# Node tables of 128 partitions, split first loads, and head sums one group later in a graph network kernel

## The reference

```python
h = relu(layernorm(x))
# first network: heads=8, head size 16
hn = layernorm(h) * g + b
fh, ft, fe = hn @ W_head.T, hn @ W_tail.T, hn @ W_ent.T
e = leaky_relu(fh[src] * ft[dst], 0.2)            # per edge
e = sum over a head's 16 of (e * attn) * log(deg[dst]) / 16
a = softmax of e over the edges of each dst
f = fe
for _ in range(5):                                 # hops
    agg = segment_sum(f[src] * a, dst)
    f = 0.85 * agg + 0.15 * fe
rst = f + h;  x = x + ff(layernorm(rst)) + rst     # ff: 128 -> 512 -> 128
# second network: three graph convolutions over the same edges with edge_weight
x = x + gcn3(relu(layernorm(x)))
```

## Time and profile before

| | |
|---|---|
| median of 3 runs | 6570.55 us |
| profiled execution | 6571.94 us |
| its span | 6570.2 us |
| granted TensorE clock, mean | 0.611 |
| PE busy | 4080.4 us, 62% |
| DVE busy | 3665.7 us, 56% |
| POOL busy | 3938.5 us, 60% |
| ACT busy | 423.4 us, 6% |
| DMA moved | 671.66 MB, 102 GB/s on average |

### The profile page before, as it was taken

One profiled execution on the slowest core, in us unless ns is written; L12 is line 12 of the kernel. 1 busy time (PEld: TensorE's weight loads), 2 busy tenths in 40 slices (PEclk: granted clock), 3 DMA queues, 4 the chain that ended last, 5 costly groups with the idle time before them and its releaser, 6 DMA issues.

```text
span 6570.2 us, 90031 instructions
## 1 busy us (share of the span) xinstructions
PE 4080.4 (62%) x19868; PEld 3634.8 (55%) x19869; DVE 3665.7 (56%) x7015; ACT 423.4 (6%) x1409; POOL 3938.5 (60%) x4073
## 2 busy tenths in 40 slices
PE   2755655625778998865555545555544555555899
PEld 1444544514668888854444534445544454544899
DVE  6765656787865555535555535555544555544211
ACT  0111111110000000000000000000000000001000
POOL 0577767711047777767777767777776777773000
PEclk9655555557965555555555555555555555566999
DMA  2345566514633323223233322332322333332576
GB/s 56 108 140 146 145 155 144 150 34 122 179 103 79 78 78 79 75 59 79 78 80 78 78 59 77 79 78 78 80 63 71 79 78 80 78 72 75 217 273 230
DMA packets 538440, 671.66 MB, mean 102 GB/s; under 512 B 102388, under 2 KB 423419, under 8 KB 528412
## 3 DMA queue, kind: packets, MB, share of 16 engines
q0 software_dynamic: 143008, 320.73, 18.8%
q1 hardware_dynamic: 391970, 345.94, 17.6%
q10 hardware_dynamic: 3418, 4.48, 0.2%
HBM read 511.17 MB, written 160.80 MB: 102 GB/s over the span
## 4 chain that ended last, share of the span: by engine, by line
POOL 30%; issue 22%; PE 21%; DMA 13%; DVE 9%; SPq 1%; DVEq 1%; ACT 1%; POOLq 0%; ACTq 0%; PEldq 0%; PEld 0%
POOL U L683 30%; DMA U<-tab_f,stage 9%; PE ps L888 7%; PE ps L1101 6%; PE ps L877 5%; DMA U<-edge_fe 2%; DVE gap L1168 2%; DVE U L1194 1%; DMA U<-tab_he,stage 1%; DVE U L1522 1%; DVE U L1494 1%; ACT stage L746 1%; DVEq L1168 1%; DVE U L1121 1%; PE ps L964 1%
## 5 line engine op out<-in xcount | busy, mean ns | idle before, releaser
L683 POOL DMA_INDIRECT U<-tab_f,stage x3224 | 3054.7, 947 | 1354.8 <-issue 865.6
L888 PE MATMUL ps<-U 128*125 128x128 f32 x8160 | 2012.3, 401 | 1075.7 <-DVE U L1194 1075.1
L888 PEld LDWEIGHTS ps<-U 128*125 128x125 f32 x8160 | 1672.7, 290 | 1209.4 <-issue 1209.1
L1194 DVE TENSOR_TENSOR U<-U,ex_it 128x512 f32<-128x512 f32 x1020 | 711.9, 698 | 1064.5 <-DMA U<-tab_f,stage 1062.9
L1145 DVE TENSOR_TENSOR U<-dloc,iota_p 128x500 f32<-128x500 f32 x1225 | 839.9, 686 | 535.0 <-DMA U<-tab_f,stage 478.0
L683 POOL DMA_INDIRECT U<-tab_he,stage x806 | 841.7, 1044 | 427.4 <-issue 244.8
L877 PE MATMUL ps<-gap 128*128 128x125 f32 x2816 | 723.9, 436 | 453.1 <-DVE gap L1168 452.5
L877 PEld LDWEIGHTS ps<-gap 128*128 128x128 f32 x2816 | 627.1, 328 | 539.7 <-DVE gap L1168 537.8
L1179 DVE SCALAR_TENSOR_TENSOR gap<-gap,U,ps 128x125 f32<-128x125 f32 x1408 | 485.6, 345 | 154.3 <-DVE gap L1179 42.6
L989 PE MATMUL ps<-U 125*128 x1632 | 422.3, 440 | 183.1 <-ACT U L783 181.3
L885 PEld LDWEIGHTS ps<-w_it,U 128*125 128x125 f32 x1632 | 439.1, 329 | 162.6 <-issue 162.5
(11 more groups left out here) (237 smaller groups left out, 2093.1 us busy)
## 6 DMA issues: line engine op xcount, KB each, us to landing
adj<-gap SPq DMA_DIRECT2D x1408, 64.0 KB
edge_fe<-U SPq DMA_DIRECT2D x204, 256.0 KB, 2.8
U<-edge_fe SPq DMA_DIRECT2D x204, 256.0 KB, 3.0
U<-tab_f,stage POOLq DMA_INDIRECT x3224, 2.5
ex_it<-adj SPq DMA_DIRECT2D x30, 1600.0 KB, 6.2
U<-adj SPq DMA_DIRECT2D x30, 1600.0 KB, 6.2
fe_a<-adj SPq DMA_DIRECT2D x15, 1600.0 KB, 6.2
U<-tab_he,stage POOLq DMA_INDIRECT x806, 3.1
```

The costliest lines, as they stand in the source:

```text
L683: pool.indirect_dma_start(to[:, k, j, :], None, table, bass.IndirectOffsetOnAxis(ap=stage[:, k, j:j + 1], axis=0)).then_inc(landed[k], 16)
L888: mm = nc.tensor.matmul(ps[0:BN, bass.ds(b * F, F)], hot[:, k, j, :], ga[:, k, j, :], start=False, stop=False, skip_group_check=True)
L1194: v.tensor_tensor(rows_, rows_, by, ALU.mult).then_inc(msgs_ready, 1)
```

## The change

Tables tab_he and tab_f get 128 x 25 rows. Row 25 p + b is now partition p of bucket b, so each partition's buckets lie together, and all 128 partitions are stored. The three that hold no node, with 29 others, are zeroed once by POOL. The source index of an edge is turned into the new row number by five more DVE operations. tab_f is stored in two parts, by SP after four banks' sums and by ACT after all seven. The copies to the sorted table and the loads of x are cut at a multiple of 16 rows; x, the constants and later the keys are loaded from ACT's queue. In the score stage a group's sum of heads is issued behind the next group's product.

```diff
-        tab_he = dram("tab_he", (N_NODES, 2 * F))
+        tab_he = dram("tab_he", (P * NB, 2 * F))
-        tab_f = dram("tab_f", (N_NODES, F))
+        tab_f = dram("tab_f", (P * NB, F))
+EVEN = BN // 16 * 16                 # 112
+EVEN_TILES = TILES // 16 * 16        # 768 of 782
+        def rows_of(table):
+            return table.rearrange("(p b) f -> p b f", p=P)
@@ sync, start
-                sp.dma_start(srt[:, k, :], of[0:TILES * P].rearrange("(t e) -> t e", e=P)).then_inc(edges_copied, 16)
-            sp.dma_start(h0[0:BN], nodes_of(a["x"])).then_inc(x_in, 16)
-            loads = [...]
-            for to, of in loads:
-                sp.dma_start(to, of, allow_slow_non_contiguous=True).then_inc(consts_in, 16)
+                for t0, t1 in ((0, EVEN_TILES), (EVEN_TILES, TILES)):
+                    sp.dma_start(srt[t0:t1, k, :], of[t0 * P:t1 * P].rearrange("(t e) -> t e", e=P)
+                                 ).then_inc(edges_copied, 16)
@@ scalar, start
+            for p0, p1 in ((0, EVEN), (EVEN, BN)):
+                act.dma_start(h0[p0:p1], nodes_of(a["x"])[p0:p1]).then_inc(x_in, 16)
+            loads = [...]
+            for to, of in loads:
+                act.dma_start(to, of, allow_slow_non_contiguous=True).then_inc(consts_in, 16)
@@ sync, keys
-            sp.wait_ge(rows_ready, 3)
+            sp.wait_ge(rows_ready, 2)
@@ sync, table
-            sp.dma_start(nodes_of(tab_he[:, 0:F]), na[0:BN]).then_inc(table_out, 16)
-            sp.dma_start(nodes_of(tab_he[:, F:2 * F]), x_sb[0:BN]).then_inc(table_out, 16)
+            sp.dma_start(rows_of(tab_he[:, 0:F]), na).then_inc(table_out, 16)
+            sp.dma_start(rows_of(tab_he[:, F:2 * F]), x_sb).then_inc(table_out, 16)
@@ key loads: the same 32 loads move from sync to scalar, before the same turns
-                        sp.dma_start(key[c * HEADS:(c + 1) * HEADS, :],
+                        act.dma_start(key[c * HEADS:(c + 1) * HEADS, :],
...
@@ sync, hop border
-                    for k in range(BANKS):
-                        b0, b1 = bank_buckets(k)
-                        sp.wait_ge(sums_out, n * BANKS + k + 1)
-                        sp.dma_start(nodes_of(tab_f)[:, b0:b1], na[0:BN, b0:b1]).then_inc(table_out, 16)
+                    b0, b1 = part_buckets(PARTS[0])
+                    sp.wait_ge(sums_out, n * BANKS + PARTS[0][1])
+                    sp.dma_start(rows_of(tab_f)[:, b0:b1], na[:, b0:b1]).then_inc(table_out, 16)
@@ scalar, hop border
             for s in range(1, HOPS):
+                b0, b1 = part_buckets(PARTS[1])
+                act.wait_ge(sums_out, s * BANKS)
+                act.dma_start(rows_of(tab_f)[:, b0:b1], na[:, b0:b1]).then_inc(table_out, 16)
                 stage_pass(s)
@@ scalar, before hop 0
-            act.dma_start(x_sb[0:BN], nodes_of(a["x"])).then_inc(x_again, 16)
+            for p0, p1 in ((0, EVEN), (EVEN, BN)):
+                act.dma_start(x_sb[p0:p1], nodes_of(a["x"])[p0:p1]).then_inc(x_again, 16)
@@ gpsimd
+            pool.wait_ge(slide_set, 1)
+            pool.memset(U[P - 32:P, 0:2 * NB * F], 0.0).then_inc(rest_set, 1)
+            pool.wait_ge(rest_set, 1)
@@ vector, row numbers
-                    v.tensor_copy(row_f[0], row_i[0]).then_inc(rows_ready, 1)
+                    link(v.tensor_copy(row_f[0], row_i[0]))
+                    link(v.tensor_scalar(row_b, row_f[0], -(BN - 1) / 2, 1.0 / BN, ALU.add, ALU.mult))
+                    link(v.tensor_scalar(row_b, row_b, ROUND, None, ALU.add))
+                    link(v.tensor_scalar(row_b, row_b, -ROUND, None, ALU.add))
+                    link(v.scalar_tensor_tensor(out=row_f[0], in0=row_b, scalar=-float(BN), in1=row_f[0], op0=ALU.mult,
+                                                op1=ALU.add))
+                    v.scalar_tensor_tensor(out=row_f[0], in0=row_f[0], scalar=float(NB), in1=row_b, op0=ALU.mult,
+                                           op1=ALU.add).then_inc(rows_ready, 1)
@@ vector, score stage
+            def reduce_scores(r, k):
+
+                dve.wait_ge(step_link, r * (3 * SLOTS) + (3 * k + 3))
+                v.tensor_reduce(ex_it[:, bass.ds(item_of(r, k), G), :],
+                                ga_wide[:, k % SLOTS, :, 0:F].rearrange("p g (h d) -> p g h d", h=HEADS),
+                                AX.X, ALU.add).then_inc(scores_done, 1)
+
                         v.tensor_tensor(heads, heads, bank(2 + k % 2).rearrange("p (g f) -> p g f", g=G),
                                         ALU.mult).then_inc(step_link, 1)
+                        if k or r0:
+                            reduce_scores(r, k - 1)
...
-                        dve.wait_ge(step_link, r * (3 * SLOTS) + (3 * k + 3))
-                        v.tensor_reduce(ex_it[:, bass.ds(item_of(r, k), G), :],
-                                        heads.rearrange("p g (h d) -> p g h d", h=HEADS),
-                                        AX.X, ALU.add).then_inc(scores_done, 1)
-
-            score_groups(0, WIN_COUNT_AT)
+
+            score_groups(0, 1)
+            score_groups(1, WIN_COUNT_AT)
...
             score_groups(FULL_ITERS, ITERS)
+            reduce_scores(ITERS - 1, SLOTS - 1)
```

66 lines of the change are left out of this document (36 added, 30 removed).

## The result

| | before | after |
|---|---|---|
| median | 6571.41 us (4 runs, 6566.51 to 6574.25) | 6490.49 us (4 runs, 6488.59 to 6491.5) |
| profiled span | 6570.2 us | 6489.3 us |
| POOL busy | 3938.5 us, 60% | 3899.4 us, 60% |
| granted TensorE clock, mean | 0.611 | 0.612 |

The ratio is 0.9876, with a 95% interval of 0.9864 to 0.9887: 81 us less (the 6570.55 us ahead of the prediction is the median of three of the four runs). I had forecast 6469 us, 102 less, with a range of 6438 to 6512.

The account below looks back on a forecast made before the run. POOL's gathers were taken as the clock of 5 of the 6.57 ms. Start -11, score stage -55, borders -33 and hop 0 -3 sum to -102 us: median 6469 us, range 6438 to 6512 (forecast alone 6440 to 6492).

Parts of the forecast that it names:

- Rival 1: Score stage: the long gather stays, by another cause or on another start; 60 us lost, 6529 us, chance 0.13.
- long compares: Score stage: three gathers slowed beside long DVE compares, said to stay long; 6 of the 70 us of slow gathering.
- Slow gathers: Score stage: reordered sums keep two-SBUF-input DVE operations off gather starts, group 5.04 instead of 5.42 us; 60 us gained.
- Look-ahead: Score stage: late sums shrink it by 3.4 of about 10 us; costs +3 at window count, +2 at first group.
- rival 2: Score stage, congested stretch: missed look-ahead lengthens each of five waits by 5.04 us; 6494 us, chance 0.12.
- Key loads on ACT: Score stage: eight issues hold ACT 2.6 us in four iterations, covered by look-ahead; taken as 0, range -12 to +12.
- The chain through ACT and PE: Score stage: product, reduction, ACT's stage and copy, PE's tails, next product; 4.53 us, under the group's 5.04.
- rival 3: Score stage: the new chain through ACT and PE becomes the clock; at 5.9 us a group 6621 us, chance 0.03.
- Borders: Four hop borders: stores from 128 partitions at 300 GB/s, 10.7 instead of 18.7 us each; -33 us (-22 to -39).
- Rival 4: Stores don't spread over more engines; borders and start give 5 instead of 44 us: 6508 us, chance 0.04.
- Start: Kernel start: DVE copies weights at 46.2 instead of 62.43 us, less added operations and later dst loads; -11 us (-13 to -5).
- Hop 0: First hop: x reloaded during its first loads, spread over all engines, delays them less; -3 us (0 to -6).

Follow-up runs that it names:

- e1: Changed kernel with each group's sum of heads back behind its own product instead of a group late: 6529.25 us, ratio 0.9930.
- e6: e1 with the next group's one-hots moved behind the product: 6605.53 us, ratio 1.0039.
- e4: Changed kernel with head sums in their own group and the leaky relu split into two operations through PSUM, neither with two SBUF inputs: 6488.17 us, ratio 0.9869.
- e5: e4 with the one-hots' column numbers also read from PSUM: 6467.56 us, ratio 0.9835.
- e2: Kernel before the change with only the sums of heads moved a group late, key loads still on SP: 6542.45 us, ratio 0.9947.
- e7: e5 with the key loads issued one pair a group instead of four pairs at a turn's start: 6454.95 us, ratio 0.9806.
- e10: Changed kernel with tab_f stored from 125 partitions instead of 128, in the same two parts on two queues: 6535.67 us, ratio 0.9937.
- e13: Changed kernel with head sums in their own group in turns 0, 7 and 25 only: 6492.96 us, ratio 0.9873.

## Why the prediction was right, and where it was off

**The mechanism.** The step on which 60 of the 102 us stood holds: a gather that starts inside one of these DVE operations with two SBUF inputs waits for its end. Three operations show it, the leaky relu in three kernels (before, e1, e6), the one-hots in e4 and the key compare, each time with the gather's end 0.82 to 0.84 us behind the operation. It goes away in e5, where one input of each lies in PSUM. Rival 1 is out. The condition was put too narrowly: the third gather of the prediction's "long compares" starts inside a tensor_scalar with one SBUF input (L1476 before, 1.95 us from 1129.39) and ends 0.82 us after it as well, and so does the gather beside L1493 above. That takes nothing from the 60 us, which came from the leaky relu.

The Trainium skill (SBUF — State Buffer, "Who interferes with whom") says that a DVE instruction with two SBUF inputs contends with an instruction of GpSimd that reads SBUF, and that one with at most one SBUF input, outside the 2-port perf modes, does not. e4 and e5 agree; whether L1493, which has one and does block, runs in such a mode, no view here shows. Its inference that descriptor generation is therefore not stalled does not hold for these gathers. Both would fit if what is held up is the reading of a gather's indices, which lie in SBUF, at its start; that for the two-input operations only the gather's start counts speaks for it, and no run here tried it.

**Slow gathers: 49 instead of 60 us.** The phases came as worked out: product at 0.32, reduction at 0.93, leaky relu at 1.52, one-hots at 2.84 after a gather's start. What was sized too low is what stays: 23.3 us instead of 10. e5 has 10.5 left with no two-input operation in its loop, for the compares and the like, where I had put 6; the other 13 come from groups out of step, where I took 4: 48 gathers of the changed kernel start inside the leaky relu, for 10.0 us, and 51 inside the one-hots, for 2.5. Groups are out of step behind each pause, while DVE catches up.

**Look-ahead: 24 instead of 5 us.** This is the step that failed, and with 19 us it is the largest part of the miss. I wrote "the other pauses are under 9 us and stay covered". I had ranked the pauses by what they cost POOL before, and the stop at turn 26 cost nothing then, so it stood in no row: it was hidden. Timeline of the changed kernel, turn 26:

```profile
757.22 2.55 PE L1027 MATMUL ps<-ident,U 128*128 128x128 f32 x11
...
759.43 0.19 ACT L733 COPY stage<-src_it 128x4 int32 x1 [4.32 <-DVE ex_it L1434]
759.81 1.33 ACT L797 COPY U<-ps 128x1408 f32<-128x1408 f32 x1 [0.19 <-PE ps L1027]
...
769.48 2.58 PE L1027 MATMUL ps<-ident,U 128*128 128x128 f32 x11 [1.51 <-ACT U L797]
...
776.27 0.69 DVE L1445 TENSOR_TENSOR U<-U,ps 128x512 f32<-128x512 f32 x1 [15.04 <-PE ps L1008]
776.87 0.68 DVE L1434 TENSOR_REDUCE ex_it<-U 128x512 f32 x1
```

PE turns four rounds of rows and DVE's product waits 15 us for the tails. With late sums the sum of the group before waits behind that product, ACT behind the sum and POOL behind ACT's stage. The rest of the 24: 2.3 at the first groups as predicted, 3.4 at the window count (predicted 3), 7.2 at turn 26 (predicted none), and 11 in the key stretch, where I had put the loads at 0 and rival 2 at 25. There e1 and e2 show 8 us for either part alone. Rival 2 was right in its place and half right in its size; the gain of SP's stores past the loads, which I had set against it, did not come. Of the five waits that I laid to the loads there, the first stands ahead of them all. For the others e7 shows that with late sums undone and ACT's queue kept they all but go when the burst does.

**Key loads on ACT: 0 taken, 8 to 10 measured** with early sums (38.5 in e1, 39.1 and 40.6 in e4 and e5, against 30.1 before), inside the 12 of the range. The eight issues stand in ACT's queue ahead of its copy and its stage.

**The chain through ACT and PE: 4.53 us predicted.** Where DVE catches up, its products follow each other in 4.5 to 4.6 us (237.86, 242.32, 246.75), against 3.8 to 4.0 before. It is under 5.04, and rival 3 stays out, but the pace at which a pause is made good is slower. e6 shows the same chain as the clock.

**Borders: 39 instead of 33 us.** The mechanism was right, the rate too low: 347 GB/s instead of the 300 that I worked out from 108/0.36. The gather came 4.4 us after ACT's issue began. Rival 4 is out. That cutting in two parts costs more than seven stores I had not seen.

**Start: 12.3 instead of 11 us.** DVE copied the weights at 46.25, predicted 46.2, and the five operations and the loads of dst took 3.9 of the 5.4 us put against it. dst did land later, and DVE's first count starts at about 36.7 instead of 33, but DVE had been waiting at the branch until 40.70 in both kernels (7.49 us idle before, 3.85 after), so that it cost nothing.

**Hop 0: 5.5 instead of 3 us,** inside its bounds.

The sum of the steps: start +1.3, borders +6.4, hop 0 +2.5 better; slow gathers 11 and pauses 19 worse, the key loads among the pauses. -102 - 10 + 30 = -82. The range of the forecast alone, 6440 to 6492, holds the time only just, and by luck: 10 us of gains that I had not counted stand against 30 us of losses, and without them it would be about 6500. The look-ahead had no bounds of its own in that range beyond rival 2. Nor is 6492 the plain sum of the worst cases that I named, +6 at the start, +11 at the borders, +12 for the key loads and +3 for hop 0, which give 6501; it takes them as not all coming together, and does not say so.

## What to carry to other kernels

When an engine's order is changed so that a buffer is freed later, list every stretch in which any engine leaves the loop, also those that cost nothing now: a pause just under the look-ahead is in no list of waits, and it is the next to be paid. A collision between two engines is better removed at its cause, here by moving one input to PSUM (6468 us), than by an order that steps around it (6490), which works only in step. A burst of loads shows in the landings of other transfers, and here pauses followed it from either queue: try to spread it over the loop, not only to move it.

## What the runs showed of the hardware

The time that PE takes for the four rounds of turn 26 depends on the granted clock in these 17 us. In the changed kernel it is at the lower level, 0.50 (1.2 GHz), and a round takes 2.58 us; in e10, whose score stage is the same code, it is 0.73 over the window from 750 to 780 us, three of four rounds take 1.39 us, and the pause of POOL is 2.68 us instead of 7.49. Timeline of e10:

```profile
765.04 1.39 PE L1027 MATMUL ps<-ident,U 128*128 128x128 f32 x11 [1.51 <-ACT U L797]
...
772.63 0.69 DVE L1445 TENSOR_TENSOR U<-U,ps 128x512 f32<-128x512 f32 x1 [10.33 <-PE ps L1008]
```

So by this pair 4.8 of the 7.5 us are the clock's. By e13, whose four rounds are all at the lower level too, early sums in the turn before take away 4.5 of them. The two overlap, as a pause is paid only beyond the look-ahead, and what the late sums cost at that place is not a fixed number. In all kernels with late sums but e10 the rounds were mostly at the lower level, in those with early ones anything from all low to all high; why is open.

A DVE operation with two SBUF inputs that starts while a gather is being issued does not lengthen it; only the start of the gather counts. In e4 the one-hots at 303.35 start 0.21 us into the gather of 303.14, which takes 0.96. For the quick one-input form this may be otherwise: L1492 starts 0.14 us into the gather of 680.09, which takes 1.15 and ends 0.12 us after it.
